# A transposing transfer of exponents in two halves, each with a wait of its own

## The chip, the cores and the metric

The kernel runs on one core of one Trainium2 chip. The metric is the device time of one execution in microseconds; the median of several runs is given.

## The reference, cut to what matters

A small perceiver block: x (2 x 256 x 512) attends to a context (2 x 4096 x 128), then passes a small attention over the heads of one token and a gated feed-forward layer. The change lies in the first attention, which the reference computes like this:

```python
q_big = apply_rope(einsum("bshk,hkq->bshq", (h @ Wq.T), w_kc_q))       # 16 heads
kv_r  = apply_rope(kv_c)                                               # 2 x 4096 x 128
q_r   = einsum("bshq,hqr->bhsr", q_big, W_qr)
k_r   = einsum("bld,hdr->bhlr", kv_r, W_kr)
attn  = softmax(einsum("bhsr,bhlr->bhsl", q_r, k_r))                   # rows of 4096
ctx_c = einsum("bhsl,bld->bhsd", attn, kv_r)
```

The key projection is absorbed into the query, so both products run against the same rotated context kv_r with 128 columns.

## The kernel before, in words

The queries are cut into tiles of 128: 2 batches x 16 heads x 2 tiles make 64 (NQT). The 4096 keys are cut into 4 chunks of 1024 (NCH), so the loop of this attention has 256 chunks (NCHUNK); the number n counts them. To keep more digits than fp16 has, the factors are split into a high and a low fp16 half, and a product is taken as hi*hi + hi*lo + lo*hi.

Five engines work on a chunk, each in its own written order, with semaphores between them:

- TensorE, `scores(n)` (L1270 to L1272): six matmuls of 128 x 512 into a PSUM slot of two banks; there are three slots. It runs five chunks ahead (AHEAD) of the weighing.
- VectorE, `chunk_maximum(n)` (L973): the maximum over the chunk.
- ScalarE, `exponents(n)` (L673): exp into `prob`, fp32. Then `take_hi(n)` (L664): the high half, fp16, into `p_both[:, n % RING, 0]`.
- VectorE, `take_lo(n)` (L962): the low half, prob less the high half, into `p_both[:, n % RING, 1]`. On VectorE the order is maximum of n+1, low half of n.
- SyncE, `turn_exponents(n)` (L398): one transposing DMA reads 128 x 2048 fp16 (both halves, 512 KB) from `p_both` and writes it as 2 x 8 blocks of 128 x 128 into `pt_both[:, n % TURNED]`. It waits until the weighing of chunk n-4 is done and the low half of n is written.
- TensorE, `weighed_keys(n)` (L1289, L1290, L1293): 16 matmuls with the transposed high half, alternately against the high and the low half of the context `kn`, then 8 with the transposed low half. It waits for the transfer before the first.

`p_both` has three buffers (RING), `pt_both` four (TURNED). ScalarE waits, before it writes the high half of n, for the transfer of n-3; VectorE, which writes the low half after the high one, needs no wait for that of its own. After each fourth chunk ScalarE also weighs the four partial sums (L679, L690). SyncE issues its DMAs in the order written; beside the exponents there are 16 transposing transfers of keys (L405, `turn_keys`), each reading 128 x 1024 fp16 (256 KB) and writing 128 x 8 x 128. Eight of them come before the loop, and eight in it, one every eighth chunk, for the second batch. After the loop it loads the weights of the later layers.

Of the kernel before, what the change touches and what calls it, by code (L numbers as in the profile page):

```python
# [57 lines left out]
RING = 3  # L58
TURNED = 4
# [3 lines left out]
def build(nc, x, ctx_kv, wq_t, w_kcq, w_qr, w_kr, w_kckv, wo_t, cos_q, sin_q, cos_k, sin_k,  # L63
          w_mix, w_gu, w_dn, s_gu, s_dn, out):
    with ExitStack() as stack:
        def sem(name):
            return stack.enter_context(nc.semaphore(name))

        def sb(st, name, shape, dt=F32):
            return st.enter_context(nc.sbuf_tensor(name, shape, dt))  # L70
# [32 lines left out]
        with ExitStack() as keys:  # L103
# [42 lines left out]
            with ExitStack() as st:  # L146
# [5 lines left out]
                p_both = sb(st, "p_both", [P, RING, 2, CHUNK], F16)  # L152
                pt_both = sb(st, "pt_both", [P, TURNED, 2, CHUNK // P, P], F16)
# [80 lines left out]
        m_done = sem("m_done")  # L234
        exp_done = sem("exp_done")
        pt_in = [sem(f"pt_in{i}") for i in range(TURNED)]
        hi_done = sem("hi_done")
        lo_done = sem("lo_done")
        pv_done = sem("pv_done")
# [57 lines left out]
        def p_hi(n):  # L297
            return p_both[:, n % RING, 0, :]

        def p_lo(n):  # L300
            return p_both[:, n % RING, 1, :]
# [30 lines left out]
        @block.sync  # L332
        def _(sp):
            def load_wq(h, i):
                sp.dma_start(wq_s[:, i, :, :].rearrange("p c k -> p (c k)"),
                             wq_t[bass.ds(h, 1), :, :].rearrange("h p n -> p (h n)")).then_inc(wq_in[i], 16)

            def load_wkcq(h, i):
                sp.dma_start(wkcq_s[:, i, :],
                             w_kcq[bass.ds(h, 1), :, :].rearrange("h p n -> p (h n)")).then_inc(wkcq_in[i], 16)  # L340

            def load_rest(h, i):
                for dst, src in ((wkckv_s, w_kckv), (wot_s, wo_t)):
                    sp.dma_start(dst[:, i, :],
                                 src[bass.ds(h, 1), :, :].rearrange("h p n -> p (h n)")).then_inc(wrest_in[i], 16)

            def load_turn(p, i):

                for m, src in ((0, cos_k), (1, sin_k)):
                    sp.dma_start(cs_k[:, i, m, :], src[:, bass.ds(p * PIECE, PIECE)]).then_inc(cs_in[i], 16)  # L350

            def load_rotated(p):

                i = p % 2
                sp.dma_start(wqr_s[:, i].rearrange("p a c r -> p (a c r)"), w_qr[p]).then_inc(wqr_in[i], 16)
                sp.dma_start(wkr_s[:, i, :], w_kr[p]).then_inc(wqr_in[i], 16)

            sp.dma_start(x_in1[:, :, :], x_v).then_inc(x_in, 16)
            load_wq(0, 0)
            load_wkcq(0, 0)  # L360
            load_rest(0, 0)
            sp.dma_start(cosq[:, :, :].rearrange("p c s -> p (c s)"), cos_q).then_inc(tab_in, 16)
            sp.dma_start(sinq[:, :, :].rearrange("p c s -> p (c s)"), sin_q).then_inc(tab_in, 16)
            load_turn(0, 0)
            load_wq(1, 1)
            load_wkcq(1, 1)
            load_rest(1, 1)
            load_rotated(0)
            load_turn(1, 1)
            load_rotated(1)  # L370

            def refill(h, i):

                sp.wait_ge(a_done, h + 1)
                load_wq(h + 2, i)
                sp.wait_ge(b_done, h + 1)
                load_wkcq(h + 2, i)
                sp.wait_ge(d_done, h + 1)
                load_rest(h + 2, i)

            for h in range(H - 2):
                refill(h, h % 2)
                if h < NP - 2:
                    sp.wait_ge(krope, 4 * (h + 1))
                    load_turn(h + 2, h % 2)
                if h >= 4 and h % 2 == 0:
                    sp.wait_ge(c_done, h - 2)
                    load_rotated(h // 2)
            sp.wait_ge(c_done, H - 4)
            load_rotated(H // 2 - 1)  # L390


            def turn_exponents(n):

                if n >= TURNED:
                    sp.wait_ge(pv_done, n - TURNED + 1)
                sp.wait_ge(lo_done, n + 1)
                sp.dma_start(pt_both[:, n % TURNED].rearrange("p a c q -> p (a c) q"),  # L398
                             p_both[:, n % RING].rearrange("p a c -> p (a c)"),
                             transpose=True).then_inc(pt_in[n % TURNED], 16)  # L400

            def turn_keys(b, p, done):

                sp.wait_ge(kn_done, b * NP + p + 1)
                sp.dma_start(kt[b][:, p].rearrange("d a (c l) -> d (a c) l", l=P),  # L405
                             kn[:, b, p].rearrange("l a k -> l (a k)"), transpose=True).then_inc(done, 16)

            for p in range(NP):
                turn_keys(0, p, kt_in[p // 2])
            for n in range(NCHUNK):  # L410
                turn_exponents(n)
                if n % 8 == 6 and 1 <= n // 8 <= NP:
                    turn_keys(1, n // 8 - 1, kt_next)


            sp.wait_ge(pv_done, NCHUNK)
            for m in range(4):
                cols = slice(m * DC * D, (m + 1) * DC * D)
                sp.dma_start(wmix[:, cols], w_mix[:, cols]).then_inc(wmix_in, 16)
            sp.wait_ge(ctx_done, NQT)  # L420
            sp.dma_start(wdn_raw[:, :, :].rearrange("p c n -> p (c n)"), w_dn).then_inc(wdn_in, 16)
            sp.dma_start(sgu[:, :, :].rearrange("p c n -> p (c n)"), s_gu).then_inc(wdn_in, 16)
            sp.wait_ge(out_full, NT)
            sp.dma_start(sdn, s_dn.partition_broadcast(P)).then_inc(wdn_in, 16)
            n = 2 * DC * P
            for j in range(HC):
                sp.dma_start(wgu_raw[:, j * n:(j + 1) * n], w_gu[:, j * n:(j + 1) * n])\
                  .then_inc(wgu_in[j], 16)
            for t in range(NT):
                sp.wait_ge(y_ok, t + 1)  # L430
                sp.dma_start(out_v[:, t, :], xres[:, t, :]).then_inc(y_out, 16)
            sp.wait_ge(y_out, 16 * NT)
# [429 lines left out]
        def _(dve):  # L862
# [95 lines left out]

            def take_lo(n):

                dve.wait_ge(hi_done, n + 1)
                nc.vector.scalar_tensor_tensor(out=p_lo(n), in0=prob[:, n % 2, :], scalar=PSCALE,  # L962
                                               in1=p_hi(n), op0=ALU.mult, op1=ALU.subtract).then_inc(lo_done, 1)
# [40 lines left out]
            for n in range(NCHUNK):  # L1004
                if n + 1 < NCHUNK:
                    chunk_maximum(n + 1)
                take_lo(n)
                if n % NCH == NCH - 2:
                    row_maximum(n // NCH)
                if n == 8:  # L1010
                    back_to_scores(2, 1 + SOON, 1 + H, 10)
# [130 lines left out]
        def _(pe):  # L1142
# [132 lines left out]
            def weighed_keys(n):  # L1275
                b, t, c = n // (NCHUNK // B), n // NCH, n % NCH
                if c == 0 and t >= 2:
                    pe.wait_ge(o_used, t - 1)
                if n < NCH:
                    pe.wait_ge(kn_done, 2 * (n + 1))  # L1280
                elif n == NCHUNK // B:
                    pe.wait_ge(kn_done, KN_DONE)
                o = ps_o[:, t % 2, c * P:(c + 1) * P]
                pe.wait_ge(pt_in[n % TURNED], 16 * (n // TURNED + 1))
                pt_hi, pt_lo = pt_both[:, n % TURNED, 0], pt_both[:, n % TURNED, 1]
                per = PIECE // P
                for k in range(CHUNK // P):
                    p, keys = 2 * c + k // per, slice(k % per * P, (k % per + 1) * P)
                    nc.tensor.matmul(o, pt_hi[:, k, :], kn[:, b, p, 0, keys], start=(k == 0), stop=False)  # L1289
                    nc.tensor.matmul(o, pt_hi[:, k, :], kn[:, b, p, 1, keys], start=False, stop=False)  # L1290
                for k in range(CHUNK // P):
                    p, keys = 2 * c + k // per, slice(k % per * P, (k % per + 1) * P)
                    last = nc.tensor.matmul(o, pt_lo[:, k, :], kn[:, b, p, 0, keys], start=False,  # L1293
                                            stop=(k == CHUNK // P - 1))
                last.then_inc(pv_done, 1)
# [318 lines left out]
```

## Time and profile before

| | |
|---|---|
| median of 3 runs | 1104.91 us (1104.62 to 1105.61) |
| profiled execution | 1106.48 us, its span 1104.7 us |
| TensorE matmul, busy | 1033.1 us (94%) |
| VectorE | 855.7 us (77%) |
| ScalarE | 799.8 us (72%) |
| GpSimd | 498.4 us (45%) |
| share of the 16 DMA engines taken by queue 1 (SyncE's) | 72.3% |
| granted TensorE clock, mean | 0.990 |

Busy time is the union of an engine's instructions over the span. The matmuls overlap one another in the records, so a sum over lines is more than the engine's busy time. Issuing a DMA and waiting on a semaphore are not busy time; they are the engine's sequencer's, marked SPq for SyncE. About 65% of the span is the loop over the 256 chunks; before it the queries are made and the context is rotated, after it come the output product, the small attention and the feed-forward layer.

### The profile page before, as it was taken

What the parts mean: (1) busy time and instruction counts of PE and PEld (TensorE: products, weight loads), DVE (VectorE), ACT (ScalarE), POOL (GpSimd) and SP (SyncE); (2) the same over time, 40 slices, a digit from 0 to 9 for tenths busy, and PEclk for the clock granted to TensorE, in tenths of its full rate; (3) what the DMA queues carried; (4) which work ended last, traced back from release to release, by engine and by line L of the source; (5) the groups of instructions that cost most, each with busy time, mean ns of one, the idle gap of its engine ahead of it and who ended that gap; (6) DMA issues with size and microseconds to landing.
All of it is one profiled execution on the core that took longest, in us unless ns stands there. A gap on an engine that the chain in (4) does not pass through costs nothing.

```text
span 1104.7 us, 24584 instructions
## 1 busy us (share of the span) xinstructions
PE 1033.1 (94%) x9456; PEld 718.9 (65%) x9456; DVE 855.7 (77%) x1177; ACT 799.8 (72%) x1380; POOL 498.4 (45%) x748
## 2 busy tenths in 40 slices
PE   4899998999999999999799999999999899999988
PEld 3444444666666677667577766776777654859877
DVE  3999888989898988888698898888898813454633
ACT  1233338899999999999799998999999932426532
POOL 1985363566767554545345454545455312000000
PEclk9999999999999999999899999999999999999989
DMA  8443365899999999999999899999998952032000
GB/s 342 132 146 114 109 138 111 180 193 204 198 202 207 207 193 199 190 188 195 192 196 193 201 179 195 192 197 194 201 193 192 192 190 105 1 132 89 1 20 20
DMA packets 568917, 180.15 MB, mean 163 GB/s; under 512 B 551520, under 2 KB 557664, under 8 KB 568160
## 3 DMA queue, kind: packets, MB, share of 16 engines
q1 hardware_dynamic: 567184, 173.33, 72.3%
q10 hardware_dynamic: 1616, 5.24, 1.5%
q8 instruction: 75, 1.23, 0.5%
q14 instruction: 42, 0.34, 0.1%
HBM read 39.07 MB, written 1.05 MB: 36 GB/s over the span
## 4 chain that ended last, share of the span: by engine, by line
PE 57%; DMA 13%; DVE 13%; ACT 10%; issue 6%; POOL 0%; SPq 0%; ACTq 0%; POOLq 0%; DVEq 0%
DMA pt_both<-p_both 13%; PE ps_o L1289 6%; PE ps_o L1290 6%; PE ps_o L1293 5%; PE ps_o L1350 5%; ACT prob L673 5%; DVE sized L973 4%; PE ps_s L1270 3%; PE ps_s L1271 3%; PE ps_s L1272 3%; DVE qcos L892 2%; DVE qrot L888 2%; ACT p_both L664 2%; PE ps_t L1270 2%; ACT oscl L690 2%
## 5 line engine op out<-in xcount | busy, mean ns | idle before, releaser
L962 DVE SCALAR_TENSOR_TENSOR p_both<-prob,p_both 128x1024 f16<-128x1024 f32 x256 | 322.3, 1259 | 87.8 <-ACT p_both L664 87.2
L664 ACT ACTIVATE p_both<-prob 128x1024 f16<-128x1024 f32 x256 | 270.6, 1057 | 34.0 <-DMA pt_both<-p_both 11.7
L1289 PE MATMUL ps_o<-kn,pt_both 128*128 128x128 f16 x2048 | 257.1, 219 | 27.9 <-DMA pt_both<-p_both 27.4
L1290 PE MATMUL ps_o<-kn,pt_both 128*128 128x128 f16 x2048 | 257.0, 219 | 0.0
L1289 PEld LDWEIGHTS ps_o<-kn,pt_both 128*128 128x128 f16 x2048 | 200.0, 98 | 71.7 <-DMA pt_both<-p_both 27.0
L973 DVE TENSOR_SCALAR_CACHE_REDUCE sized<-ps_s,against 128x1024 bf16<-128x1024 f32 x170 | 217.0, 1276 | 0.0
L1290 PEld LDWEIGHTS ps_o<-kn,pt_both 128*128 128x128 f16 x2048 | 200.7, 98 | 24.7
L673 ACT ACTIVATE prob<-ps_s,nmax,unscale 128x1024 f32<-128x1024 f32 x170 | 204.4, 1202 | 11.9 <-DVE sized L973 11.8
L538 POOL TENSOR_TENSOR osum<-oscl 128x256 f32<-128x256 f32 x64 | 47.9, 749 | 257.9 <-ACT oscl L690 257.9
L1293 PE MATMUL ps_o<-kn,pt_both 128*128 128x128 f16 x2048 | 156.6, 219 | 0.0
L1270 PE MATMUL ps_s<-kt,q_hi 128*128 128x512 f16 x340 | 129.3, 380 | 3.5 <-ACT prob L673 2.6
L1271 PE MATMUL ps_s<-kt,q_hi 128*128 128x512 f16 x340 | 129.1, 380 | 0.0
L1272 PE MATMUL ps_s<-kt,q_lo 128*128 128x512 f16 x340 | 128.9, 379 | 0.0
L1293 PEld LDWEIGHTS ps_o<-kn,pt_both 128*128 128x128 f16 x2048 | 125.5, 98 | 0.0
L973 DVE TENSOR_SCALAR_CACHE_REDUCE sized<-ps_t,against 128x1024 bf16<-128x1024 f32 x86 | 109.8, 1277 | 0.0
L673 ACT ACTIVATE prob<-ps_t,nmax,unscale 128x1024 f32<-128x1024 f32 x86 | 103.4, 1202 | 7.2 <-DVE sized L973 7.1
L529 POOL TENSOR_TENSOR lrec<-lsum,minus 128x1 f32<-128x1 f32 x64 | 96.0, 1500 | 5.3
L453 POOL TENSOR_TENSOR rstd<-mv,mhalf 128x1 f32<-128x1 f32 (+1 forms) x9 | 7.3, 816 | 152.2 <-DVE mv L1001 145.2
L690 ACT ACTIVATE oscl<-ps_o,weigh 128x128 f32<-128x128 f32 x256 | 71.9, 360 | 5.5 <-issue 5.5
L596 ACT COPY qhk<-ps_t 128x512 f32<-128x512 f32 x16 | 9.4, 586 | 85.7 <-PE ps_t L1161 85.7
L1270 PE MATMUL ps_t<-kt,q_hi 128*128 128x512 f16 x172 | 65.3, 379 | 2.7 <-ACT prob L673 1.5
L513 POOL CAST q_hi<-q_raw 128x128 f16<-128x128 f32 x64 | 59.3, 926 | 16.8 <-PE ps_t L1272 6.8
(215 smaller groups left out, 1849.8 us busy)
## 6 DMA issues: line engine op xcount, KB each, us to landing
wgu_raw<-w_gu_dram SPq DMA_DIRECT2D x11, 512.0 KB, 10.0
wq_s<-wq_t_dram SPq DMA_DIRECT2D x16, 256.0 KB, 3.8
wot_s<-wo_t_dram SPq DMA_DIRECT2D x16, 256.0 KB, 2.8
kvr<-ctx_kv_dram ACTq DMA_DIRECT2D x4, 1024.0 KB, 12.4
pt_both<-p_both SPq DMA_TRANSPOSE x256, 3.8
kvr<-w_mix_dram SPq DMA_DIRECT2D x4, 1024.0 KB, 9.2
wkcq_s<-w_kcq_dram SPq DMA_DIRECT2D x16, 192.0 KB, 2.4
wdn_raw<-w_dn_dram SPq DMA_DIRECT2D x1, 2816.0 KB, 8.9
```

The source lines that it names most:

```text
L529: nc.gpsimd.tensor_tensor(lrec[:, i, :], lsum[:, i, :], minus[:, :], ALU.pow).then_inc(row_ok, 1)
L664: nc.scalar.mul(p_hi(n), prob[:, n % 2, :], PSCALE).then_inc(hi_done, 1)
L673: nc.scalar.activation(prob[:, n % 2, :], flat(slot(n)), ACT.Exp, bias=nmax[:, i, c:c + 1], scale=unscale[:, h:h + 1], accum_out=rsum[:, i ...
L690: last = nc.scalar.mul(oscl[:, i, c, :], ps_o[:, i, c * P:(c + 1) * P], weigh[:, i, c:c + 1])
L962: nc.vector.scalar_tensor_tensor(out=p_lo(n), in0=prob[:, n % 2, :], scalar=PSCALE, in1=p_hi(n), op0=ALU.mult, op1=ALU.subtract).then_inc( ...
L973: nc.vector.tensor_scalar(sized[:, n % 2, :], flat(slot(n)), against[:, h:h + 1], None, ALU.mult, ALU.min, accum_out=nmax[:, i, c:c + 1]). ...
L1270: nc.tensor.matmul(o, q_hi[:, t % 2, :], hi, start=True, stop=False)
L1271: nc.tensor.matmul(o, q_hi[:, t % 2, :], lo, start=False, stop=False)
L1272: last = nc.tensor.matmul(o, q_lo[:, t % 2, :], hi, start=False, stop=True)
L1289: nc.tensor.matmul(o, pt_hi[:, k, :], kn[:, b, p, 0, keys], start=(k == 0), stop=False)
L1290: nc.tensor.matmul(o, pt_hi[:, k, :], kn[:, b, p, 1, keys], start=False, stop=False)
L1293: last = nc.tensor.matmul(o, pt_lo[:, k, :], kn[:, b, p, 0, keys], start=False, stop=(k == CHUNK // P - 1))
```

## The change

Each chunk's transfer becomes two. The first moves the high half and waits for the high half alone (`hi_done`, ScalarE); the second moves the low half and waits for `lo_done` (VectorE). Each is a transposing DMA of 128 x 1024 fp16, 256 KB. The first counts up the old semaphore of the buffer, the second a new one, `pt_low_in`. TensorE waits for the first transfer where it waited before, and for the second ahead of the eight low matmuls. ScalarE's wait before writing the high half of n is in its words the same, but is now for the high transfer of n-3; VectorE gets a wait of its own for the low transfer of n-3, before it writes the low half.

```diff
+        pt_low_in = [sem(f"pt_low_in{i}") for i in range(TURNED)]
...
                 if n >= TURNED:
                     sp.wait_ge(pv_done, n - TURNED + 1)
+                sp.wait_ge(hi_done, n + 1)
+                sp.dma_start(pt_both[:, n % TURNED, 0], p_hi(n), transpose=True).then_inc(pt_in[n % TURNED], 16)
                 sp.wait_ge(lo_done, n + 1)
-                sp.dma_start(pt_both[:, n % TURNED].rearrange("p a c q -> p (a c) q"),
-                             p_both[:, n % RING].rearrange("p a c -> p (a c)"),
-                             transpose=True).then_inc(pt_in[n % TURNED], 16)
+                sp.dma_start(pt_both[:, n % TURNED, 1], p_lo(n), transpose=True).then_inc(pt_low_in[n % TURNED], 16)
...
             def take_lo(n):
 
+                if n >= RING:
+                    dve.wait_ge(pt_low_in[(n - RING) % TURNED], 16 * ((n - RING) // TURNED + 1))
                 dve.wait_ge(hi_done, n + 1)
...
                     nc.tensor.matmul(o, pt_hi[:, k, :], kn[:, b, p, 1, keys], start=False, stop=False)
+                pe.wait_ge(pt_low_in[n % TURNED], 16 * (n // TURNED + 1))
                 for k in range(CHUNK // P):
```

## Rows read from the trace of the kernel before

**Rows 1.** Timeline, ends of the loop (start us, duration us, engine, line); L1293 by source.

```profile
175.52 25.19 SPq L398 DMA_TRANSPOSE pt_both<-p_both  x9
...
206.40 1.57 SPq L398 DMA_TRANSPOSE pt_both<-p_both  x1
...
885.04 1.69 SPq L398 DMA_TRANSPOSE pt_both<-p_both  x1
...
L1293 PE MATMUL ps_o<-kn,pt_both x2048: 219/219/314, 181.8 to 890.1; 128*128 128x128 f16 x187
```

**Rows 2.** Windows, the loop: busy us of each engine, clock, DMA share, GB/s.

```profile
175.52:889.50 713.98, 681.05 (x7652) 489.26 (x7651) 622.72 (x833) 659.15 (x1088) 384.11 (x655) 1.00 0.98 194
```

**Rows 3.** Timeline of TensorE, the eight low matmuls that close three successive chunks.

```profile
602.37 0.61 PE L1293 MATMUL ps_o<-kn,pt_both 128*128 128x128 f16 x8
...
605.01 0.61 PE L1293 MATMUL ps_o<-kn,pt_both 128*128 128x128 f16 x8
...
607.64 0.61 PE L1293 MATMUL ps_o<-kn,pt_both 128*128 128x128 f16 x8
```

**Rows 4.** Waits, whole span: us in total, times, longest.

```profile
PE ps_o L1289 <- DMA pt_both<-p_both: 27.4, 31, 6.9
...
ACT p_both L664 <- DMA pt_both<-p_both: 11.7, 13, 6.1
```

**Rows 5.** Timeline of one late transfer; landings of the three issued in 455 to 462.

```profile
453.58 1.06 ACT L664 ACTIVATE p_both<-prob 128x1024 f16<-128x1024 f32 x1
454.67 1.22 DVE L962 SCALAR_TENSOR_TENSOR p_both<-prob,p_both 128x1024 f16<-128x1024 f32 x1 [1.12 <-ACT p_both L664]
...
455.97 1.62 SPq L398 DMA_TRANSPOSE pt_both<-p_both  x1
...
458.31 2.62 SPq L398 DMA_TRANSPOSE pt_both<-p_both  x1
...
461.10 0.22 PE L1289 MATMUL ps_o<-kn,pt_both 128*128 128x128 f16 x1 [0.26 <-DMA pt_both<-p_both]
...
461.99 0.22 PE L1293 MATMUL ps_o<-kn,pt_both 128*128 128x128 f16 x1
...
DMA to landing us min/median/max: 3.7/4.5/5.0
```

**Rows 6.** Line L398, all exponent transfers: ns of the issue min/median/max; landings.

```profile
L398 SPq DMA_TRANSPOSE pt_both<-p_both x256: 1553/1643/8248, 175.5 to 885.0; - x128
...
DMA to landing us min/median/max: 3.6/3.8/11.8
```

**Rows 7.** Waits of the sync queue before exponent issues: total us, times, longest.

```profile
SPq L398 <- PE ps_o L1293: 219.0, 216, 3.4
...
SPq L398 <- DVE p_both L962: 19.7, 4, 12.0
```

**Rows 8.** Key transfers: line L405, all; landings; those inside the loop; timeline of eight.

```profile
L405 SPq DMA_TRANSPOSE kt<-kn x16: 1290/1332/1494, 152.4 to 375.6; - x16
...
DMA to landing us min/median/max: 3.2/3.3/4.5
...
L405 SPq DMA_TRANSPOSE kt<-kn x8: 1302/1336/1373, 219.1 to 375.6; - x8
...
152.37 11.09 SPq L405 DMA_TRANSPOSE kt<-kn  x8
```

**Rows 9.** The reload of x on ScalarE's queue: timeline, and its DMA row.

```profile
538.21 0.41 ACTq L697 DMA_DIRECT2D xres<-x_dram  x1
...
xres<-x_dram ACTq DMA_DIRECT2D x1, 1024.0 KB, 10.8
```

**Rows 10.** Windows: eight key transfers back to back; one chunk of the loop.

```profile
152.37:163.46 11.09, 10.49 (x38) 5.02 (x37) 9.40 (x14) 3.81 (x10) 6.08 (x5) 1.00 1.01 207
600.00:602.64 2.64, 2.64 (x34) 1.93 (x32) 1.63 (x3) 2.55 (x6) 1.82 (x5) 1.00 0.99 225
```

## The prediction

> **What bounds the kernel now.** I read the page's busy shares, then the windows of the attention stage, the waits, and last the rows of single transfers, because the change touches only the loop over 256 chunks. That loop lasts from the first exponent transfer at 175.52 us to the last low-half matmuls at 890.1 us [rows 1]. In the 713.98 us window TensorE is busy 681.05 us, ScalarE 659.15, VectorE 622.72, and the DMA engines show a share of 0.98 [rows 2]. So TensorE is the first bound, and three others stand close behind it. Its own pace is plain: the blocks of eight low matmuls that close a chunk start at 602.37, 605.01 and 607.64 us [rows 3], 2.635 us apart. 256 chunks at that pace are 675 us, and the stage takes 714, or 2.79 a chunk. What is missing is mostly waiting: TensorE stood 27.4 us for the transposed exponents, in 31 places, the longest 6.9 us [rows 4]. This is the time that the change could give back.
>
> **The transfer as it is.** The high half is written by ScalarE in 1.06 us (from 453.58), the low half by VectorE in 1.22 us (from 454.67), the transfer is issued at 455.97 [rows 5]. From its issue it takes 3.8 us to land (median), of which the sync queue itself is held 1.643 us (median; 1.553 at least) [rows 6]. That queue does nothing else in the loop but eight key transfers. Its share of the stage: from 175.5 to the end of the last issue at 886.7 are 711.2 us; idle before exponent issues 219.0+19.7 us, less the 12.0 us of the first one, which lies before the stage [rows 7], so 226.7 idle. The queue is occupied for 484 us, 474 of them for exponent issues when 8 x 1.34 for keys are taken off. 256 x 1.643 would be 421, so 53 us are stretched issues. One is shown: of three transfers one lands 5.0 us after its issue and another 3.7; it is that of 455.97, for TensorE, waiting for it, starts at 461.10, and the next issue, at 458.31, holds the queue 2.62 us [rows 5]: an issue is held back while the transfer before it is late.
>
> **What a transfer of half the size costs.** The change replaces one 512 KB transfer by two of 256 KB (128 x 1024 fp16). The trace has that very shape: the key transfers of L405 read 128 x 1024 fp16 and write 128 x 8 x 128, as each new transfer does. They land in 3.3 us (median), and they hold the queue 1.332 us (median), 1.290 at least; those issued among exponent transfers during the loop 1.336, 1.302 at least [rows 8]. Halving the data takes only 0.31 us off the issue; about 1.0 us is fixed. Eight of them issued back to back took 11.09 us, so 1.386 us each with the wait between [rows 8].
>
> **Part by part.**
> High half: it no longer waits for VectorE's 1.22 us and lands in 3.3 instead of 3.8 us, so if the queue is free it is there 1.3+0.5 = 1.8 us earlier. Low half: issued when the queue has finished with the high one, 1.39 us after it, so about 0.1 us later than the whole one is issued now, and landing after 3.3: 0.4 us earlier than now. Its first use lies behind sixteen matmuls, which take about 0.9 us (from 461.10 to 461.99 [rows 5]). So each deadline alone is relaxed by over 1 us. That is the gain side.
> The queue: per chunk 2 x 1.386 = 2.77 us of issuing, against 1.643 now and against TensorE's 2.635. This is the term that decides. 256 x 2.77 + 8 x 1.386 = 709.6 + 11.1 = 720.7 us of pure issuing, without one pause. It starts when the first high half is written, 1.3 us before 175.52, at 174.2, so the queue is free at 894.9; the last low transfer was issued 1.39 before, at 893.5, lands at 896.8, and its eight matmuls add about 0.8 (0.61 and the last one's end): 897.6 against 890.3 now: **+7 us**.
> Pauses that issuing now hides and then no longer can: (a) the first chunks come slowly, for reasons ahead of the queue: 206.40-175.52 = 30.9 us for ten chunks [rows 1] against 27.7: **+3**. (b) The reload of x at 538.21 us goes through the same DMA engines, 1024 KB landing in 10.8 us [rows 9]; one exponent issue is stretched to 8.248 us [rows 6], 6.6 more than usual: **+7**. (c) The other stretched issues, 53 less 6.6 = 46 us. Now they fall into the queue's free time; with the queue full they add. But the engines get more room: the data of a chunk now come every 2.77 us and not at times every 2.34 (455.97 to 458.31). Bounds 0 and 46; I take **+20**, somewhat under half, since a stretched issue follows a late transfer and the late ones remain.
> The two waits on the engines: VectorE's new wait before the low half of chunk n is for the low transfer of n-3, which with issues 2.77 apart landed some 3 us earlier (8.3 us lie between the two, and it needs 1.2 to be written, 0.1 to be issued and 3.3 to land); behind it on VectorE stand the next maximum and with it exp. If the queue falls behind, this wait and ScalarE's (L664, 11.7 us now [rows 4]) are how the engines are slowed, and no further cost. TensorE's new wait in mid-chunk costs nothing when met: between scores and exponents stands such a wait now, and chunks still close 2.635 apart. When not met, what stands behind it is the low matmuls and the next scores; that is where the queue's lateness will show. More issuing on SP delays nothing else, except the eight key transfers (needed only at chunk 128) and w_mix after the loop, which waits for the last chunk anyway. The rest after 890 us shifts whole.
> Sum: +7+3+7+20 = **+37 us**. The profiled execution took 1106.48 us, 1.8 around its span of 1104.7; that becomes 1143.5. The median of the runs is 1.6 lower, 1104.91, and so 1142.
>
> A page of the Trainium skill speaks against this reckoning. "DMA: Bandwidth & Descriptors", section "Issuing engines are not separate DMA queues", says that the sequencer time to start a DMA is usually small beside the DMA. Here it is 1.33 of 3.3 us by the rows; by that rule the queue would not count and the result would be that of the second rival below. The same page, "Rules for kernel authors", advises to issue early and wait late, which the change does, and also to join small transfers into large ones, which it undoes.
>
> **Rivals.**
> 1. The queue just keeps up. If issues beside other work go at the lowest seen, 1.29 with 0.05 between (2.68 a chunk), issuing sums to 697, 24 us less than above; with the same pauses the end comes at +37-24 = +13, and with few stretched issues at -7. For it: the present pace, 2.79 a chunk, is not under 2.77. Against: the eight issues amid the loop took 1.336 in the middle [rows 8]. Time 1098 to 1118.
> 2. Faster: the cost of an exponent half is shared out by size (0.82 us each), so the queue has room and only latency counts. Then most of TensorE's 27.4 us of waiting goes, but not the 6.9 us beside the reload: -20, 1085 us. For it: every other number of the loop. Against: the key rows. It decides at 2 x (issue + gap) under 2.635, an issue under 1.26 us.
> 3. The DMA engines become the bound. While the eight key transfers ran back to back their share was 1.01, with 207 GB/s; in a chunk with one transfer it is 0.99 with 225 GB/s [rows 10]. If a half occupies the engines for the whole 1.386 us, nothing is left to catch up a late one: all 46 us of stretches add, +63, and half as much again if one late transfer holds two issues: +86. That is 1168 to 1191. Against: the back-to-back landings do not drift, 3.2 to 4.5 us, median 3.3 [rows 8].
>
> **How the numbers follow.** Chances: queue-bound as reckoned, +15 to +63 (1120 to 1168), 0.62; rival 1, 0.14; rival 2, 0.10; rival 3, 0.14. The likeliest is 1142; its own range is 1120 to 1168. The range for 8 in 10 takes in two thirds of rival 1 and of rival 3: 1105 to 1184; left out are rival 2 with 0.10, and a third each of rivals 1 and 3 with 0.09. The median can be told from no change by about 0.2%, 2.2 us. Faster: rival 2 and a quarter of rival 1, 0.13; same: 0.03; slower: 0.84.
>
> **What would show it.** Right: the sync queue's idle time before exponent issues falls from 227 us to nearly nothing, the exponent issues are 512 in number, 1.33 us each, chunks close 2.77 us or more apart; TensorE waits mainly at the first low matmul (L1293's group), for the low transfer, and its share falls to some 90%. VectorE's or ScalarE's waits for pt_both grow. Wrong: issues clearly under 1.3 us, or queue idle time over 50 us with a longer loop. Then latency, or the engines, was the matter. If the transfers land later than 3.3 us while issues stay at 1.33, rival 3 holds.

## The result and the profile after

The changed kernel takes 1168.76 us (median of 4 runs, 1165.25 to 1171.63) against 1105.26 beside it: ratio 1.0559, 95% interval 1.053 to 1.0589. It is slower by 63.5 us, where 37 were forecast.

Of the page of the changed kernel: the span, the busy shares, the sync queue's row, q1 (packets, MB, share of the 16 DMA engines), and the chain that ended last, by engine.

```profile
span 1167.0 us, 25093 instructions
...
PE 1048.1 (90%) x9456; PEld 721.7 (62%) x9456; DVE 855.1 (73%) x1177; ACT 800.7 (69%) x1380; POOL 470.7 (40%) x748
...
q1 hardware_dynamic: 575376, 173.36, 74.2%
...
PE 39%; DMA 17%; SPq 14%; DVE 14%; ACT 10%; issue 6%; POOL 0%; DVEq 0%; ACTq 0%; POOLq 0%
```

No engine has more to do than before: VectorE and ScalarE are busy within 1 us of the old figures, TensorE has as many matmuls (x9456), and the sync queue moves the same bytes (173.36 MB against 173.33). TensorE's share fell from 94 to 90%, though it is busy 15 us longer (1048.1 against 1033.1); the loop's granted clock is 0.99 against 1.00 and there are more waits to start anew from, and how much each makes of the 15 us was not separated. New in the chain is SPq, the sync queue's issuing, with 14%; before it had 0.

The loop now, in one window [rows 2 answers to it]:

```profile
173.96:950.90 776.94, 696.37 (x7674) 492.06 (x7673) 623.51 (x834) 661.07 (x1090) 356.32 (x655) 0.99 0.98 179
```

Its last exponent issue, from the timeline of SyncE, and its last low matmuls, by their line (the last two times are those of the first and the last start) [rows 1].

```profile
947.17 1.32 SPq L401 DMA_TRANSPOSE pt_both<-p_both  x1
```

```profile
L1297 PE MATMUL ps_o<-kn,pt_both x2048: 219/219/314, 181.5 to 950.5; 128*128 128x128 f16 x187
```

The last low matmul starts at 950.5 instead of 890.1 us: 60 of the 62 us by which the spans differ lie in the loop. The rest, 2 us, came after it; its cause is open. The queue's exponent issues by line, high half (L399) and low half (L401), with the landings of each [rows 6 and 8 are their like]:

```profile
L399 SPq DMA_TRANSPOSE pt_both<-p_both x256: 1231/1256/5043, 174.0 to 945.9; - x128
...
DMA to landing us min/median/max: 2.7/2.8/8.3
...
L401 SPq DMA_TRANSPOSE pt_both<-p_both x256: 1231/1311/3078, 175.2 to 947.2; - x128
...
DMA to landing us min/median/max: 2.8/2.9/7.7
```

And how they stand in the queue, from the timeline of SyncE alone (start us, us):

```profile
643.50 1.25 SPq L399 DMA_TRANSPOSE pt_both<-p_both  x1
644.80 1.31 SPq L401 DMA_TRANSPOSE pt_both<-p_both  x1
646.21 1.25 SPq L399 DMA_TRANSPOSE pt_both<-p_both  x1
647.50 1.31 SPq L401 DMA_TRANSPOSE pt_both<-p_both  x1
648.91 1.25 SPq L399 DMA_TRANSPOSE pt_both<-p_both  x1
650.21 2.09 SPq L401 DMA_TRANSPOSE pt_both<-p_both  x1
652.40 1.25 SPq L399 DMA_TRANSPOSE pt_both<-p_both  x1
```

This is a full queue. An undisturbed chunk takes it 646.21 - 643.50 = 2.71 us: two issues and 0.045 + 0.10 us between. By their ends the issues come evenly, 1.355 us apart in the median for both halves: ahead of a high half there are two waits and not one, the gap is 0.055 us longer, and the issue is shorter by the same 0.055 us (1.256 against 1.311). The pieces of the loop then are 256 x 2.71 = 694 us, eight key transfers with 11 us, and what the issues took beyond their medians, 66 us by the trace's records (their sum is 723.0, 256 x (1.256 + 1.311) would be 657). That is 771 of the 774.5 us from the first issue at 174.0 to the end of the last at 948.5. The other 4 are pauses. In the records all 256 halves of each kind were complete before their issue began, 236 of the low ones by 2.4 us or more, and the weighing of n-4, which frees the buffer, was over by at least 2.3 us: the data and the buffer waited for the queue, not the queue for them.

The waits, whole span (total us, times, longest) [rows 4]:

```profile
ACT p_both L665 <- DMA pt_both<-p_both: 66.1, 69, 4.6
...
DVE p_both L965 <- DMA pt_both<-p_both: 48.1, 40, 2.8
PE ps_o L1292 <- DMA pt_both<-p_both: 45.0, 43, 4.8
...
PE ps_o L1297 <- DMA pt_both<-p_both: 30.2, 31, 2.7
```

Every consumer waits more: TensorE 27.4 -> 75.2 us, part of it now in mid-chunk (L1297); ScalarE 11.7 -> 66.1, VectorE nothing -> 48.1. The two producers' waits are how a late queue slows the rest.

**The stretched issues.** The issue at 650.21 is one, 2.09 us. The DMA view of the 2.4 us around it (649.9 to 652.3) gives busy tenths and GB/s in 40 slices of 0.06 us, then the queues; the last line is queue 1's in the quiet 5.9 us before it (644.0 to 649.9). A share can be over 100%, since a packet that starts in the window counts whole.

```profile
DMA  0090499999999990000000001001000100899999
GB/s 0 0 273 21 115 213 260 282 265 269 277 269 132 43 4 0 0 0 0 0 0 0 0 13 21 9 9 13 9 9 9 13 9 13 183 277 286 299 290 286
...
q1 hardware_dynamic: 913, 0.23, 115.0%
q8 instruction: 1, 0.02, 3.3%
...
q1 hardware_dynamic: 4634, 1.15, 86.4%
```

From about 650.8 to 651.9 us next to nothing moves. Then the flow comes back. What the quiet stretch does not have is a packet of queue 8, an instruction fetch of 16 KB on one of the engines; it starts at 650.0 us and lasts 1.3. In the quiet stretch the engines' share is 0.86, so they have pauses. Queue 8 in the whole loop, in the changed kernel and in the one before:

```profile
q8 instruction: 60, 0.98, 0.7%
...
q8 instruction: 60, 0.98, 0.6%
```

Beside the 60 packets stand 61 exponent issues over 1.5 us. By the records 59 of the 61 overlap such a packet, and of the other 451 issues only 30 do. In the kernel before the tie is looser: 79 issues lie over 0.25 us above their median, and 46 of them, with two thirds of the excess, overlap a packet; what stretched the others was not followed. There a stretched issue fell into the queue's free time, 227 us of it by the wait rows [rows 7], 217 by the issues' own records.

A caution on reading the wait rows of SyncE: after the change they still name 54.6 and 53.4 us of waiting before L401 and L399, though the gaps between the issues sum to 41 us, all but 5 of it the 0.045 and 0.10 us steps. A release that falls inside a stretched issue is taken there for the end of a wait. The timeline decides.

### The profile page after: what moved, and what is told of

It is laid out like the page before. It is cut to its first block, busy times and chain, and to the rows that moved or that the text cites. A ratio compares the mean times of both kernels' runs of the same rounds, so it can differ in the third digit from the quotient of the medians.

```text
span 1167.0 us, 25093 instructions
## 1 busy us (share of the span) xinstructions
PE 1048.1 (90%) x9456; PEld 721.7 (62%) x9456; DVE 855.1 (73%) x1177; ACT 800.7 (69%) x1380; POOL 470.7 (40%) x748
## 3 DMA queue, kind: packets, MB, share of 16 engines
q1 hardware_dynamic: 575376, 173.36, 74.2%
## 4 chain that ended last, share of the span: by engine, by line
PE 39%; DMA 17%; SPq 14%; DVE 14%; ACT 10%; issue 6%; POOL 0%; DVEq 0%; ACTq 0%; POOLq 0%
DMA pt_both<-p_both 17%; SPq L401 7%; SPq L399 7%; PE ps_o L1354 5%; ACT prob L674 4%; PE ps_o L1297 3%; DVE p_both L965 3%; ACT p_both L665 3%; PE ps_o L1292 3%; PE ps_o L1293 3%; DVE sized L976 2%; DVE qcos L893 2%; DVE qrot L889 2%; PE ps_s L1273 2%; PE ps_s L1274 2%
## 5 line engine op out<-in xcount | busy, mean ns | idle before, releaser
L965 DVE SCALAR_TENSOR_TENSOR p_both<-prob,p_both 128x1024 f16<-128x1024 f32 x256 | 318.8, 1245 | 144.7 <-ACT p_both L665 95.7
L665 ACT ACTIVATE p_both<-prob 128x1024 f16<-128x1024 f32 x256 | 270.6, 1057 | 83.0 <-DMA pt_both<-p_both 66.1
L1293 PE MATMUL ps_o<-kn,pt_both 128*128 128x128 f16 x2048 | 257.4, 220 | 0.0
L1293 PEld LDWEIGHTS ps_o<-kn,pt_both 128*128 128x128 f16 x2048 | 201.1, 98 | 24.7 <-issue 0.6
L1297 PE MATMUL ps_o<-kn,pt_both 128*128 128x128 f16 x2048 | 157.7, 220 | 30.9 <-DMA pt_both<-p_both 30.2
L539 POOL TENSOR_TENSOR osum<-oscl 128x256 f32<-128x256 f32 x64 | 50.5, 789 | 320.4 <-ACT oscl L691 320.4
L1297 PEld LDWEIGHTS ps_o<-kn,pt_both 128*128 128x128 f16 x2048 | 122.9, 98 | 40.1 <-DMA pt_both<-p_both 38.4
L1273 PE MATMUL ps_t<-kt,q_hi 128*128 128x512 f16 x172 | 65.7, 382 | 2.1 <-ACT prob L674 1.2
L1274 PE MATMUL ps_t<-kt,q_hi 128*128 128x512 f16 x172 | 65.7, 382 | 0.0
L1275 PE MATMUL ps_t<-kt,q_lo 128*128 128x512 f16 x172 | 65.7, 382 | 0.0
```

Source lines behind the costliest of these rows:

```text
L665: nc.scalar.mul(p_hi(n), prob[:, n % 2, :], PSCALE).then_inc(hi_done, 1)
L1273: nc.tensor.matmul(o, q_hi[:, t % 2, :], hi, start=True, stop=False)
L1274: nc.tensor.matmul(o, q_hi[:, t % 2, :], lo, start=False, stop=False)
L1275: last = nc.tensor.matmul(o, q_lo[:, t % 2, :], hi, start=False, stop=True)
```

## The experiments

Ratios are to the kernel before, run beside it on the same chip.

**How many chunks are split.** The first three experiments split only some chunks and move the others as before.

```diff
+        def split(n):
+            return n % 4 == 0
...
+                if split(n):
+                    sp.wait_ge(hi_done, n + 1)
+                    sp.dma_start(pt_both[:, n % TURNED, 0], p_hi(n), transpose=True).then_inc(pt_in[n % TURNED], 16)
...
+                else:
+                    sp.wait_ge(lo_done, n + 1)
+                    sp.dma_start(pt_both[:, n % TURNED].rearrange("p a c q -> p (a c) q"),
...
-                pe.wait_ge(pt_low_in[n % TURNED], 16 * (n // TURNED + 1))
+                if split(n):
+                    pe.wait_ge(pt_low_in[n % TURNED], low_count(n))
```

VectorE's wait for the low transfer is left out in the same chunks. In the second experiment the condition is n % 2 == 0, in the third n % 4 != 3.

> Only the chunks with n % 4 == 0 are moved in two transfers (the high one early); the other three in one as before. Theory Q (the sync queue is the bound of the changed kernel; an issue held back by a late DMA engine costs only where the queue has no free time): the queue needs 3 x 1.69 + 2.71 = 7.8 us for four chunks against TensorE's 10.54, so nothing is lost, and chunk 4j, which comes latest (10.7 us of TensorE's waits in the kernel before are for these chunks), gains up to 1.8 us of landing: 1096 to 1106 us. Rival E (each split costs its share, through the DMA engines or the waits, whatever the queue's free time): 63.5/4 = +16, so 1121 us. Rival W (only the added waits cost): +16 too.

> Only the chunks with n % 2 == 0 are moved in two transfers. Theory Q: the queue needs 2 x 1.69 + 2 x 2.71 = 8.8 us for four chunks, 1.7 us free, more than one stretch of about 1.1 us: still 1095 to 1108 us. Rival E: half of 63.5, 1137 us.

> All chunks but n % 4 == 3 are moved in two transfers. Theory Q: the queue needs 1.69 + 3 x 2.71 = 9.8 us for four chunks, 0.7 us free under TensorE's 10.54. A stretched issue of about 1.1 us in every four chunks is then only partly hidden: +0 to +25 us, 1105 to 1130. The step from here to the changed kernel is the largest. Rival E: three quarters of 63.5, 1153 us.

| split | ratio | 95% | median us | exponent issues, sum us |
|---|---|---|---|---|
| none | 1 | | 1107.78 | 484 |
| a quarter | 0.9942 | 0.9922 to 0.9962 | 1101.4 | 541 |
| half | 0.9962 | 0.9942 to 0.9981 | 1104.07 | 592 |
| three quarters | 1.0043 | 1.0021 to 1.0066 | 1112.52 | 658 |
| all | 1.0559 | 1.053 to 1.0589 | 1168.76 (beside 1105.26) | 723 |

All three came out in the ranges of theory Q. A cost per split would give +16, +32, +48 us; measured are -6, -4, +5, and then +57 for the last quarter. That is a resource that has room until it is full. It settles against rival E and against any price of a split by itself. The issues' sum grows evenly, by 51 to 66 us a step. The time between issues shrinks, by the records from 217 us to 154, 106, 48 and 41, and of the last 41 only 5 are more than the fixed steps. So the first steps are hidden, the third in part, and the last not at all. Below the limit the early landing is worth what the change meant it to be: with a quarter split TensorE's wait at the first high matmul falls from 27.4 us to:

```profile
PE ps_o L1306 <- DMA pt_both<-p_both: 17.7, 17, 3.2
```

This kernel is faster than the changed one and, by 0.58%, than the one before.

**Two transfers, neither early.**

```diff
-                sp.wait_ge(hi_done, n + 1)
+                sp.wait_ge(lo_done, n + 1)
                 sp.dma_start(pt_both[:, n % TURNED, 0], p_hi(n), ...)
-                sp.wait_ge(lo_done, n + 1)
                 sp.dma_start(pt_both[:, n % TURNED, 1], p_lo(n), ...)
```

> Two transfers for every chunk, but both are issued after the low half is written, so nothing starts earlier than in the kernel before. Theory Q: the queue's work is the same as in the changed kernel, 2.71 us a chunk and the stretches; once it is behind, it never waits for a half: 1165 to 1175 us, the same as the changed kernel. Rival T (the early start itself costs, since the high transfer collides with work of others at that time): clearly faster than the changed kernel, 1110 to 1140. If earliness had still helped the changed kernel, this one would be slower by up to 1.3 us a chunk, 1200 and more.

1169.44 us, ratio 1.0561 (1.0524 to 1.0599), the same as the changed kernel. With the queue behind, the early wait buys nothing, and it costs nothing either. The issues sum to 722 us here and 723 in the changed kernel.

**The waits alone.** One transfer as before, and the two added waits on its semaphore.

```diff
+                if n >= RING:
+                    dve.wait_ge(pt_in[(n - RING) % TURNED], 16 * ((n - RING) // TURNED + 1))
                 dve.wait_ge(hi_done, n + 1)
...
+                pe.wait_ge(pt_in[n % TURNED], 16 * (n // TURNED + 1))
                 for k in range(CHUNK // P):
```

> The kernel before with its one transfer per chunk, and the two added waits of the change placed as the change places them, on the one transfer's semaphore (VectorE before the low half of n on the transfer of n-3, TensorE ahead of the eight low matmuls on the transfer of n). Theory Q: both are met when they are reached and cost nothing: 1104 to 1110 us, no difference. Rival W (the waits themselves stall VectorE and TensorE, 256 times some 0.1 us or more): +25 us or more.

1111.99 against 1107.77 us, ratio 1.0046 (1.0015 to 1.0078): a little slower and 2 us outside the range, where no difference was expected. So each wait was tried by itself.

> Of the two added waits only TensorE's, ahead of the eight low matmuls, on the one transfer's semaphore, which has been met already. With both waits the kernel before was 0.46% slower (1112.0 against 1107.8 us), where I had expected nothing. If TensorE's wait is the cause: +3 to +6 us here (an instruction more between matmuls, some 10 to 20 ns a chunk of it on the path). If VectorE's is: no difference, within 2 us.

> Of the two added waits only VectorE's, ahead of the low half, on the transfer of n-3 (met already, since ScalarE has waited for it before the high half). If VectorE's wait is the cause of the 0.46%: +3 to +6 us here; otherwise no difference. If both this and the run with TensorE's wait show none, the 0.46% were a matter of placement or of that chip's spread, and stay unexplained.

TensorE's: 1.001 (0.9994 to 1.0025), no difference told. VectorE's: 1.0022 (1.0007 to 1.0037), about 2.4 us, somewhat less than the 3 to 6 that were named for it as the cause. In the kernel before the waits cost a few us at most, and VectorE's is the likelier part; why a wait that is met should cost there is not settled. Of the 63.5 us they need not have any, since the queue's own pieces fill the loop.

**Less work for TensorE.** The eight matmuls per chunk of the high exponents with the low half of the context are left out, once in the changed kernel, once in the kernel before.

```diff
                     nc.tensor.matmul(o, pt_hi[:, k, :], kn[:, b, p, 0, keys], ...)
-                    nc.tensor.matmul(o, pt_hi[:, k, :], kn[:, b, p, 1, keys], ...)
```

> The changed kernel without the eight matmuls per chunk of the high exponents against the low half of the context (that product is left out), 16 instructions of TensorE's 60 in a chunk. TensorE's own pace is then some 0.45 us a chunk faster, 115 us in all. Theory Q: TensorE is not the bound; the queue's 2.71 us a chunk stay. Stretched issues belong to the fetching of instructions on one of the 16 DMA engines (61 packets of 16 KB in the loop, 61 issues over 1.5 us): with about a quarter fewer instructions about 45 of each, some 15 to 20 us less: 1145 to 1155 us. Rival B (the queue is held back by its own backlog of transposed data, not by fetches): 61 stretches stay and 1165 to 1170 us. Rival P (TensorE's pace still counts in the changed kernel): 1050 to 1100 us.

> The kernel before with the same eight matmuls per chunk left out. With TensorE out of the way the next bound shows: the queue needs 1.69 us a chunk; ScalarE's own order gives 2.34, 2.34, 2.60 and 3.55 us in four chunks where nothing disturbs it, 2.71 a chunk. Theory: 1085 to 1100 us, set by ScalarE, and shorter than the changed kernel with the same cut by 50 us or more. If the queue mattered here too, it would not be shorter than 1140.

The changed kernel with fewer matmuls: 1154.65 us, ratio 1.044 (1.0379 to 1.0502), 14 us less than with all of them and in the range of the theory of the fetches. Its loop in one window, its high issues, and queue 8 in that window:

```profile
175.00:936.00 761.00, 616.29 (x5606) 386.76 (x5604) 622.60 (x834) 660.63 (x1089) 356.18 (x655) 0.97 0.96 182
```

```profile
L399 SPq DMA_TRANSPOSE pt_both<-p_both x256: 1231/1256/5215, 175.0 to 933.2; - x128
...
q8 instruction: 44, 0.72, 0.5%
```

TensorE is busy 80 us less and the loop ends only some 12 us earlier; TensorE's pace did not set it. The issues' medians are unchanged (1.256, and 1.308 for the low halves). What fell is the number of fetches in the loop, from 60 to 44 (the expectation's 61 and 45 are one too many), and with it that of issues over 1.5 us, from 61 to 47; the time beyond the medians fell from 66 to 52 us. These 14 us are the whole difference between the two loops. That is what the theory of the fetches asked for, and rival B did not. The pages also tell whose fetches they are: with 4096 of TensorE's instructions left out (25093 to 20997 in all) queue 8 has 16 packets less (75 to 59 in the whole span), one for 256 instructions. The granted clock is lower here, 0.965 against 0.987 over the span, and the kernel is the faster one all the same, so the clock did not set the time. It is not excluded that something else about the fewer matmuls helped.

The kernel before with fewer matmuls, a single run: 1103.85 us, hardly less than with all of them (1107.77), where 1085 to 1100 were expected. In its waits a new one has come up; the second line is its loop in one window:

```profile
PE ps_s L1270 <- ACT prob L673: 46.9, 71, 2.1
...
175.00:890.00 715.00, 605.65 (x5640) 379.91 (x5639) 622.91 (x834) 662.87 (x1096) 383.18 (x655) 0.99 0.94 196
```

TensorE, with 75 us less to do in the loop, waits for ScalarE to free a score slot, and for the transfers 39.7 us instead of 27.4. ScalarE is busy 662.87 of 715 us. So behind TensorE stood another bound of almost the same height, and freeing TensorE gave next to nothing. That ScalarE alone is this bound is not shown: in the chain that ended last VectorE has 23% beside ScalarE's 29%.

**The fixed part of an issue.** Four transfers of 128 KB a chunk.

```diff
+                half = CHUNK // 2
+                blocks = half // P
...
-                sp.dma_start(pt_both[:, n % TURNED, 0], p_hi(n), transpose=True).then_inc(pt_in[n % TURNED], 16)
+                for m in range(2):
+                    sp.dma_start(pt_both[:, n % TURNED, 0, m * blocks:(m + 1) * blocks],
+                                 p_hi(n)[:, m * half:(m + 1) * half],
+                                 transpose=True).then_inc(pt_in[n % TURNED], 16)
...
```

The low half is treated the same way, and the waiting engines count 32 to a chunk and not 16.

> Four transfers of 128 KB per chunk, two for each half, the waits as in the changed kernel. It measures the fixed part of an issue. 512 KB hold the queue 1.64 us, 256 KB 1.28 on average; if that is fixed + size, 128 KB hold it 1.10, with the gaps 1.16, four of them 4.6 us a chunk, and the time is 174 + 256 x 4.6 + 11 + 216, some 1580 to 1650 us. If the cost went by size alone, or by the DMA engines' data, the time would stay at 1169.

1799.44 us (a single run), 150 above the upper end. Issues of the high half and of the low half, and queue 1 on the page (packets, MB, share of the 16 DMA engines):

```profile
L402 SPq DMA_TRANSPOSE pt_both<-p_both x512: 1188/1267/2544, 174.0 to 1575.2; - x171
...
L407 SPq DMA_TRANSPOSE pt_both<-p_both x512: 1188/1267/2524, 176.5 to 1577.8; - x171
...
q1 hardware_dynamic: 591760, 173.43, 43.9%
```

Half the data saves next to nothing more: the issue takes 1.27 us for 128 KB, 1.26 to 1.31 for 256 KB, 1.64 for 512 KB, and from end to end it is 1.310 us for 128 KB against 1.355 for 256 KB. My line through two points, fixed plus size, was wrong below 256 KB; there the issue is nearly all fixed. The 1024 issues sum to 1333 us, the gaps to 61 and the eight key transfers' issues to 10.5, in all the 1405 us of the loop (174 to 1579). The bytes are the same and their share of the DMA engines is down to 43.9%, so it is issues, not bytes, that fill the time.

**Which quarter is split.**

> As the run that splits only n % 4 == 0 (0.58% faster than before), but the split chunks are n % 4 == 2. If the gain comes from the early landing of the chunk that ScalarE makes latest (n % 4 == 0, after it has weighed four partial sums), it is gone here: 1104 to 1110 us, ratio 0.998 to 1.003. If any early high half gives it (more room for a late landing anywhere): 0.994 again.

Ratio 0.9982 (0.9972 to 0.9993), against 0.9942 for n % 4 == 0. The two intervals do not meet, so most of the gain belongs to the chunk that comes after ScalarE's weighing of four sums. A small part is left when another chunk is split; only n % 4 == 2 was tried. The range given for the first case, 0.998 to 1.003, just holds it.

## Why the prediction came out as it did

Direction and mechanism held: the queue is the bound, its chunk costs it two issues, and the engines are slowed through the waits for pt_both. The size was off by 26 us. The measured 1168.8 lies 0.8 us above the range given to the forecast case (1120 to 1168), where that of rival 3 begins, and inside the whole range (1105 to 1184), so the time alone does not tell the two cases apart; the experiments do. In the terms of the sum the loop came to -9 +4 +4 +62 = +61 us, where +7 +3 +7 +20 were forecast. Two errors of opposite sign stand in it, so that the total is nearer than its largest term is luck.

- Issue time of a half: forecast 1.386 with its gap, 2.77 a chunk; measured 1.355 and 2.71. The key transfers [rows 8] were the right row, 0.03 us high each. Pure issuing was forecast at 720.7 us and came to 705: 16 us too much, which turns +7 into -9. That about 1.0 us of an issue is fixed was too low; by the four transfers it is some 1.27.
- Slow first chunks (a), +3: about 4 us of pauses in the whole loop, 2 of them in the first four chunks. About right.
- Reload of x (b), +7: the longest issue is 5.04 us instead of 8.25, 3.8 over its median. Slightly too much.
- **The other stretched issues (c), +20 of at most 46: this is the term that was mis-sized.** Measured are 66 us beyond the medians, 62 without the reload. That is above its own upper bound. Two things were wrong in it. The 53 us that I worked out from the queue's idle time [rows 7] were low: the issues' own records give 63 for the kernel before. And I took under half, reasoning that the engines would have more room at 2.77 us a chunk. They have, but here it did not help: a stretched issue comes with an instruction fetch, one in 12 to 13 us in both kernels, and each costs the queue about 1.0 us (62 by 60). Only much more room went with less: with four transfers, queue 1's share at 43.9%, the same 60 fetches cost some 0.8 us each. The stretches' sum was nearly the same as before, 66 us against 63; only its cover was gone. "The late ones remain" stood in the text, and the number did not follow it.
- The added waits, costed at nothing: 0 to a few us in the kernel before (ratio 1.0046 together), and none that the changed kernel's loop has room for.
- "So TensorE is the first bound" of the kernel before: too simple. With TensorE relieved it stayed at 1103.85 us. This changed nothing in the sum, but it bears on rival 2. The gain in reach was not 20 us; the best split gave 6.
- Of the signs, the queue's idle time, the pace of the chunks and the producers' waits came as written. Two did not. TensorE waits mainly at the first high matmul, not at the first low one (45.0 against 30.2 us). And issues clearly under 1.3 us were to show the forecast wrong, yet the high ones take 1.256 in a full queue; what counts is the issue with its gap.

The rivals. 1, the queue just keeps up: its condition, 2.68 us a chunk, was nearly met (2.71), and still it was far off, since without any free time stretches add up whatever the pace. 2, the issue's cost shared out by size: excluded by the issue rows and by the four transfers. 3, the DMA engines as the bound: its time, 1168 to 1191, fits at the low end, its mechanism does not. Their share was 0.98, but in the undisturbed stretch 0.86, transfers landed in 2.8 to 2.9 us and not later than the 3.3 forecast, and with 1024 issues for the same bytes the time grew by 630 us. The time of queue 1's packets did grow with the change, from 799 us (72.3% of 1104.7) to 866 (74.2% of 1167.0), but with four transfers it is 789 (43.9% of 1797.6), so it is not what the bytes need. What rival 3 had right is the sentence that a late transfer is never caught up; the reason is the queue, not the engines.

On the rule of the Trainium skill ("DMA: Bandwidth & Descriptors", section "Issuing engines are not separate DMA queues"), that the time to initiate a DMA is usually small beside the DMA: the trace does not agree for transposing transfers of this size, where the issue takes 1.26 to 1.31 of the 2.8 to 2.9 us to landing, and here the issuing set the pace of the loop.

## What to carry to other kernels

Before splitting a transfer, count what its issuing costs the queue: issues per iteration times the issue's duration, found on the nearest transfer of the new size, against the iteration's time. What matters is not only that the sum stays below, but that the free time covers the disturbances too; here 0.7 us free in four chunks was already too little, 1.7 enough (both are estimates from 1.69 and 2.71 us of queue time against 10.54 of TensorE's). Split where lateness hurts (one chunk in four gave 0.58%), not everywhere. A high share of an engine says little about whether relieving it helps, until the next bound is known.

## What was not expected of the hardware

- A transposing issue on the sync queue hardly gets shorter below 256 KB: 1.27 us for 128 KB, 1.26 to 1.31 for 256 KB, 1.64 for 512 KB in median. From end to end in a full queue it is 1.310 us for 128 KB and 1.355 for 256 KB.
- One 16 KB instruction fetch on the DMA engines goes with about 1 us in which the queue's issue stands and nearly no transposed data move (0 to 21 GB/s instead of some 280). 60 fetches and 61 stretched issues in the changed kernel, 44 and 47 with fewer matmuls. That one engine's delay holds up the other fifteen is read from the flow; how is not shown.
- The low halves' issues take 1.311 us and the high ones' 1.256, for the same shape and size, also when both are issued at the same point (1.312 and 1.255). It is no difference of the halves: the gap ahead of the high one is longer by the same 0.055 us, and the ends stay 1.355 us apart. With four transfers the first of a chunk, behind the longer gap, takes 1.211 and the other three 1.27, again with even ends. So in a full queue the second wait, which is met, costs nothing. Why the ends keep this pace is not shown.
